# A graph-attention block on one core: the loads of the edge slots written out, with four table entries per register read

## The reference, cut to what matters

```
# N = 1250 nodes, D = 768, 4 heads of C = 192, 3 layers; 41250 edges (src, dst), sorted by dst
loops = arange(N); src, dst = edges plus loops
x1 = relu(x @ W_ah + b_ah)
for each of 3 layers:                                   # gat_conv
    h    = (x1 @ W).reshape(N, 4, 192)
    as_n = (h * a_src).sum(-1);  ad_n = (h * a_dst).sum(-1)
    e    = leaky_relu(as_n[src] + ad_n[dst], 0.2)
    p    = exp(e - segment_max(e, dst)[dst])
    out  = segment_sum(p / segment_sum(p, dst)[dst] * h[src], dst) + b     # then relu
y = relu(concat(3 layers) @ W_out + b_out)
return layernorm(x + y)
```

## Time and profile before

| | |
|---|---|
| median of 3 runs | 987.62 us (987.02 to 990.31) |
| profiled execution, its own time | 989.36 us |
| its span, first to last instruction | 987.1 us |
| mean granted TensorE clock | 0.993 of full speed |
| PE busy | 946.7 us (96% of the span) |
| DVE busy | 742.9 us (75%) |
| ACT busy | 367.7 us (37%) |
| POOL busy | 52.3 us (5%) |

### The profile page before, as it was taken

How to read it: one execution, slowest core, us unless ns; L and a number is a source line. 1 busy time by engine, 2 the same in 40 slices (tenths; PEclk the granted TensorE clock), 3 DMA queues, 4 the chain that set the end, 5 groups by cost and what they waited for, 6 DMA issues and landing times. The chain is left out here.

```text
span 987.1 us, 15188 instructions
## 1 busy us (share of the span) xinstructions
PE 946.7 (96%) x5662; PEld 874.0 (89%) x5662; DVE 742.9 (75%) x1076; ACT 367.7 (37%) x534; POOL 52.3 (5%) x107
## 2 busy tenths in 40 slices
PE   6778899999999999999999999999999999999997
PEld 2556654999999999999999999999999869999996
DVE  6768898699999759997997998988878273234223
ACT  1444532221222234555555465465465461001000
POOL 3333000000000000001001000000010000000000
PEclk9998999999999999999999999999999999999999
DMA  5233272255344381316218136138632173323201
GB/s 167 38 85 87 66 253 77 91 163 157 102 155 136 108 240 54 87 45 130 91 39 166 55 87 121 52 90 262 215 91 66 52 191 112 122 79 109 79 32 31
DMA packets 56347, 108.14 MB, mean 110 GB/s; under 512 B 12669, under 2 KB 39902, under 8 KB 55143
## 3 DMA queue, kind: packets, MB, share of 16 engines
q1 hardware_dynamic: 37460, 66.17, 22.1%
q0 software_dynamic: 5744, 18.82, 8.7%
q10 hardware_dynamic: 13090, 22.44, 7.3%
HBM read 80.34 MB, written 27.08 MB: 109 GB/s over the span
## 5 line engine op out<-in xcount | busy, mean ns | idle before, releaser
L1308 PE MATMUL ps<-R_W 125*125 125x193 f32 x2400 | 397.8, 327 | 5.1 <-ACT R_XIN L720 3.9
L1308 PEld LDWEIGHTS ps<-R_W 125*125 125x125 f32 x2400 | 391.2, 188 | 8.7 <-ACT R_XIN L720 7.6
L705 ACT ACTIVATE R_W<-R_EXP,s 125x1250 f32<-125x1250 f32 x120 | 161.5, 1347 | 161.9 <-PE ps L1308 93.8
L995 DVE SCALAR_TENSOR_TENSOR R_W<-R_W,R_CNT 125x1250 f32<-125x1250 f32 x120 | 174.6, 1455 | 4.3 <-DVE R_EXP L984 2.3
L954 DVE CUSTOM_DVE_ANT_0 R_ROWS<-R_MASK,R_ROWS 125x1250 bf16<-125x1250 bf16 x100 | 138.5, 1456 | 3.2 <-ACTq L658 3.2
L1225 PE MATMUL ps<-Wl_hi,x_hi 128*125 128x384 f32 x360 | 122.1, 339 | 0.0
L1225 PE MATMUL ps<-Wl_hi,x_lo 128*125 128x384 f32 x360 | 121.6, 338 | 0.0
L1225 PE MATMUL ps<-Wl_lo,x_hi 128*125 128x384 f32 x360 | 121.5, 338 | 0.0
L1367 PE MATMUL ps<-Wo_hi,xs_hi 128*125 128x384 f32 (+2 forms) x324 | 109.5, 338 | 0.3 <-PE ps L1357 0.3
L1367 PE MATMUL ps<-Wo_lo,xs_hi 128*125 128x384 f32 (+2 forms) x324 | 109.5, 338 | 0.0
L1367 PE MATMUL ps<-Wo_hi,xs_lo 128*125 128x384 f32 (+2 forms) x324 | 109.2, 337 | 0.0
(11 more groups left out here) (149 smaller groups left out, 898.3 us busy)
## 6 DMA issues: line engine op xcount, KB each, us to landing
xs_dram<-R_XIN POOLq DMA_DIRECT2D x18, 625.0 KB, 10.5
h_dram<-R_HOUT ACTq DMA_DIRECT2D x30, 336.0 KB
R_W<-h_dram SPq DMA_DIRECT2D x12, 840.0 KB
R_ROWS<-as_dram SPq DMA_DIRECT2D x12, 625.0 KB, 4.5
R_EXP<-u_dram SPq DMA_DIRECT2D x6, 1250.0 KB, 6.5
R_X<-u_dram SPq DMA_DIRECT2D x6, 1250.0 KB, 5.7
R_ROWS<-in_W_all SPq DMA_DIRECT2D x18, 384.0 KB, 3.6
Wo_sb<-in_W_out POOLq DMA_DIRECT2D x1, 6912.0 KB, 27.3
```

Of the source, the lines that this page charges most:

```text
L705: nc.scalar.activation(prob[r % PSLOTS], expo[:, r % XSLOTS], ACT.Exp, bias=s02[:, r % NT, ds(2 * p + r // NT, 1)]).then_inc(S["exp_done"], 1)
L995: nc.vector.scalar_tensor_tensor(out=prob[r % PSLOTS], in0=prob[r % PSLOTS], scalar=HUGE, in1=cntT[:, r % NT, 0:N], op0=ALU.min, op1=ALU.m ...
L1308: ins = mm(ps[0:PT, o:o + HW], prob[r % PSLOTS][:, t * PT:(t + 1) * PT], hB[:, q, j], start=(j == 0 and t % 2 == 0), stop=(j == NT - 1), s ...
```

## The change

`load_slot` and its loops are replaced by `load_slots`, which is written out: for each four windows one instruction reads four entries of `table` into four registers, without a check of their values, and then four DMAs follow; no queue loop is left. A batch is now a triple (first, mid, last): SP loads the windows up to mid, POOL the rest. There are seven batches, of 4, 8, 12, 16, 20, 24 and 21 windows, of which SP loads 4, 4, 8, 8, 12, 16 and 12 (64 in all, 52 before) and POOL 0, 4, 4, 8, 8, 8 and 9 (41, before 53). POOL's loads now stand ahead of its 20 `iota`. There are three one-hot buffers instead of two; they fill the space that was kept free at the start of R_EXP and a little more, and `stage_more` moves to R_ROWS.

```diff
-BATCHES = [(0, 4), (4, 8), (8, 16), (16, 28), (28, 40), (40, 54), (54, 70), (70, 88), (88, NW)]
-ONES = 2
+BATCHES = [(0, 4, 4), (4, 8, 12), (12, 20, 24), (24, 32, 40), (40, 52, 60), (60, 76, 84), (84, 96, NW)]
+ONES = 3
...
-        o = KT * HALF
...
-        stage_more, o = view(R_EXP, o, PT, (NT, PT), f16)
...
+        stage_more, _ = view(R_ROWS, o, PT, (NT, PT), f16)
...
-        def load_slot(eng, w, signal):
-
-            start = eng.value_load(table[0:1, ds(w, 1)], min_val=0, max_val=EDGES)
-            eng.dma_start(e8[:, ds(w, 1)].rearrange("p o i s -> p (o i s)"),
-                          edges[ds(start, SLOT)].rearrange("(p i) s -> p (i s)", i=CPW)).then_inc(signal, 16)
+        def load_slots(eng, kind, w0, w1, signal):
+
+            for a in range(w0, w1, 4):
+                z = min(a + 4, w1)
+                _, places = nc.values_load_multi_w_load_instructions(
+                    table[0:1, a:z], engines=[kind], min_val=0, max_val=EDGES,
+                    skip_runtime_bounds_check_because="...")
+                for w, place in zip(range(a, z), places):
+                    eng.dma_start(e8[:, w:w + 1].rearrange("p o i s -> p (o i s)"),
+                                  edges[ds(place, SLOT)].rearrange("(p i) s -> p (i s)", i=CPW)).then_inc(signal, 16)
...
-            for i, (w0, w1) in enumerate(BATCHES):
-                with sp.Fori(w0, (w0 + w1) // 2) as w:
-                    load_slot(sp, w, win_in[i])
+            for i, (w0, mid, w1) in enumerate(BATCHES):
+                load_slots(sp, mybir.EngineType.SP, w0, mid, win_in[i])
...
+            pool.wait_ge(S["table_sb"], 1)
+            for i, (w0, mid, w1) in enumerate(BATCHES):
+                load_slots(pool, mybir.EngineType.Pool, mid, w1, win_in_pool[i])
...
...
-                dve.wait_ge(win_in[i], 16 * ((w0 + w1) // 2 - w0))
-                dve.wait_ge(win_in_pool[i], 16 * (w1 - (w0 + w1) // 2))
+                dve.wait_ge(win_in[i], 16 * (mid - w0))
+                if mid < w1:
+                    dve.wait_ge(win_in_pool[i], 16 * (w1 - mid))
```

More of the change, by code:

```diff
@@ L37 @@
 BLOCKS = CPW // EPR * 2
-BATCHES = [(0, 4), (4, 8), (8, 16), (16, 28), (28, 40), (40, 54), (54, 70), (70, 88), (88, NW)]
-WIDEST = max(z - a for a, z in BATCHES)
-ONES = 2
+BATCHES = [(0, 4, 4), (4, 8, 12), (12, 20, 24), (24, 32, 40), (40, 52, 60), (60, 76, 84), (84, 96, NW)]
+WIDEST = max(z - a for a, m, z in BATCHES)
+ONES = 3
 RING = 250
@@ L334, in acc_cols @@
             return ps[0:PT, o:o + MC]
-        def load_slot(eng, w, signal):
-            start = eng.value_load(table[0:1, ds(w, 1)], min_val=0, max_val=EDGES)
-            eng.dma_start(e8[:, ds(w, 1)].rearrange("p o i s -> p (o i s)"),
-                          edges[ds(start, SLOT)].rearrange("(p i) s -> p (i s)", i=CPW)).then_inc(signal, 16)
+        def load_slots(eng, kind, w0, w1, signal):
[3 more added lines that the diff above has]
+                    table[0:1, a:z], engines=[kind], min_val=0, max_val=EDGES,
+                    skip_runtime_bounds_check_because="the table holds EDGES less GE times a count of groups, 0 to EDGES / GE")
+                for w, place in zip(range(a, z), places):
+                    eng.dma_start(e8[:, w:w + 1].rearrange("p o i s -> p (o i s)"),
+                                  edges[ds(place, SLOT)].rearrange("(p i) s -> p (i s)", i=CPW)).then_inc(signal, 16)
         @block.sync
@@ L523, in _ @@
             ins.then_inc(S["consts_made"], 1)
[L525 to L528, removed]
             pool.wait_ge(S["h_ps"], NT * (PARTS - 1))
```

## The result

The changed kernel takes 964.45 us (median; 963.98 to 965.66), the kernel before 987.63 in the same comparison (987.02 to 990.31): a ratio of 0.9762, with a 95% interval of 0.9742 to 0.9782, so 23.2 us less. The forecast was 965.5.

A forecast was written before the change was run, and what follows sets the result against it. PE was taken to bound all from the scores on, slot-load loops the stage before. Gains of 16.2 (waits), 5.6 (clock) and 1.3 (idle) make 23.1, less 1.0: 987.6 - 22.1 = 965.5 us; range 963 to 968.5, 8 in 10 962.8 to 972.

The forecast's parts named there:

- The bound: From the scores' start at 154.63 us PE bounds everything, busy 818.6 of 832.5 us; the gain is that start's move.
- The cadence: Slot loads in the counting stage: written out, SP issues one per 0.67 us instead of 1.51, POOL 0.85 instead of 1.53.
- The bound from static DMAs, 0.44: Lower limit for SP's time per slot load, 0.44 us, from three static DMAs in a row in 1.31.
- Rival A: Slot loads: SP's cadence is 0.9 to 1.25 us; at 1.0 gain 16, 971 us; at 1.25 gain 2, 985; chance 0.11.
- The rule on register loads: Table reads for slot loads: some 200 ns per register even in bulk, 0.15 more per slot, cadence an estimated 0.82 us.
- PE's need: Counting stage with slots always there: PE needs 71.5 us of the present 93.34, without 16.2 of waits and 5.6 half-clock excess.
- The third buffer: One-hot buffers at changes of batch: a third covers small PE waits, in all 0 to 3 us, counted inside the 71.5.
- Two batches fewer: Counting stage: saves DVE 2.1 us, which PE's work hides, so worth nothing by itself.
- After the units: Between last unit and scores: PE arrives at 131.5, last by 0.9 after DVE's 130.6; scores' start gains 23.1 us.
- Rival C: Behind the faster stage, x's second part is late and PE's clock falls: 3 to 6 of 22 us lost, 970; chance 0.07.
- Rival B: Slot loads: SP stays at 1.51 us a slot with 64 slots, last one-hot 12.4 us slower, 1000 us; chance 0.04.
- Rival D: Slot loads: landings, not issues, were late, so the change does nothing, 987 us; chance 0.02.

The follow-up runs named there:

- the version with moved instructions: The changed kernel with four of DVE's five small integer instructions after batch 0 moved to after batch 3: 964.49 us, run again 964.96 us.
- the kernel with the checked loads: The changed kernel with the loop's body written out, per slot one entry read with its bounds check, then the DMA: 977.86 us, ratio 0.9891.

## Why the prediction was right

- **The bound.** The step that put the whole gain at the start of the scores held: 832.47 us behind it before, 832.44 after.
- **The cadence.** Taken 0.67 on SP, measured 0.64, and 0.67 on POOL, where 0.85 was taken. The bound from static DMAs, 0.44, and the price of one shared read were the right rows. Rival A, 0.9 or more, is ruled out by it.
- **The rule on register loads** did not apply. The trace has 0.302 us for four entries against 0.268 for one, 0.03 for three registers more. By the figure of the Trainium skill ("Runtime: NRT & Kernel Launch", Instruction fetch mechanics) they would cost an estimated 0.6; that page speaks of registers loaded from HBM, and `table` lies on the chip, which the prediction passed over.
- **PE's need.** Predicted 71.5 plus 1.0 of small waits, measured 71.42 with 1.5 of waits in it. Two parts were off and met: PE's busy time fell by 7.2 us (77.14 to 69.90), where the three half-clock stretches account for 5.6. The other 1.6 goes with the waits: in stages without a half-clock stretch PE's busy time is 69.71 with one wait, 69.90 with two, 70.38 with three, 71.31 with nine and 72.04 with eleven, so each wait lengthens it by some 0.2 us on top of its own idle time.
- **The third buffer.** This is the term that was mis-sized: I held it at 0 to 3 us, because I set DVE's 2.4 to 2.7 us against two whole units. It is worth some 6 us (0.9833 to 0.9762 or 0.9769, 0.985 to 0.9792). When DVE has filled its second buffer, PE has been at work on the first for as long as that took. An estimate from the prediction's own numbers: 2 x 1.36 - 1.1 = 1.6 us are left with two buffers and 3.0 with three, against 2.4 to 2.7; units without an x1 step leave less. The sum was not hurt, since the third buffer was in it; the expectation for the writing out alone was, by 4 us.
- **Two batches fewer** were put at nothing. With three buffers they are worth about 2 us; 1.2 of it is seen in the stage (71.33 against 70.14), the rest was not separated.
- **After the units.** PE was to be last at the scores by 0.9, with no idle time. DVE was last, and PE idled 0.49: PE's x1 steps ended at 129.5 and not at 131.5, since the units had ended at 93.4, and DVE's products at 129.8, with a wait of 1.1 us for weights in them. x1's second part was not late, and no wait of PE for it shows. Rival C did not happen.
- **Rival B** was right as a mechanism: with the loop's cadence the new split is 13.0 us slower (1000.8), where 12.4 and 1000 were worked out.
- **Rival D** was right for one wait, the longest, and the sentence "by their loops and not by their bytes" is wrong there. DVE's 4.81 us before 74.25 ended with SP's slot of 67.8:

```profile
L339 SPq DMA_DIRECT2D R_EXP<-in_edges x1: 345/345/345, 67.8 to 67.8; - x1
DMA to landing us min/median/max: 6.5/6.5/6.5
```

ACT had issued x's second part at 67.11. With 1.9 us the slot would have landed at 69.7, and DVE was free at 69.44: some 4.6 of the 12.8 us were the landing's. In the changed kernel SP has issued all its slots by 55.0 and ACT issues this load at 56.36, so the faster cadence also took the slots out of its way. No run moves that load alone with the loops kept, so what that would give is open.
- **Luck.** The forecast did not have PE's start at 21.98 (23.86 before), but little of it reaches the end. With the new batches, three buffers and the new cadence the last unit ended at 93.4 and 93.8 for starts at 21.98 and 21.99, and at 93.8 to 94.2 for starts from 23.80 to 24.10; in the kernel before it ended at 117.2 and 115.3 for starts at 23.86 and 23.99, set by the slots. The 24.7 us between the first two profiles are instead large because the profile before was of an execution 1.7 us above the median. In the timed runs the gain was 23.2 against 22.1. The stage's 71.4 us against 71.5 plus 1.0 is luck in part: 69.9 of work, 1.6 under the forecast, and 1.5 of waits, half a microsecond over it.

## What to carry to other kernels

Before a queue's DMAs are blamed for their bytes, divide the time of a run of issues by its count and compare that with the DMA instruction's own row: here 1.51 against 0.35 us said that the loop around it was the cost. Then work out for each batch by when its data is wanted, and from that the cadence that suffices. Look at the landings too: a small load that goes out just behind a large one can take three times as long (6.4 and 6.5 us here against 1.9), and no cadence shows that. A second edit such as a buffer may be worth nothing before the first and a quarter of the gain after it. Size buffers by what is left in them at the moment the producer turns to other work, and by the consumer's short stretches, and not by their number times its mean.

## What was not expected of the hardware

- PE's ten x1 steps between the edge table and unit 0 (20 matmul records) took 8.65, 9.82, 9.95, 10.02, 10.35, 11.33 or 11.40 us in the profiles, and half clock accounts for the difference. Where they took 10.35 the granted clock is 0.5 for a stretch that begins at 13.6 to 14.2 and ends at 17.0 to 17.6; 3.4 us at half clock cost the 1.7. Where they took 9.82 to 10.02, or 11.33 and 11.40, the views print 1.00, but matmuls and weight loads take up to twice as long (0.34 us for a weight load, 0.19 later) until 16.1 or until 19.2 to 19.4. The traces of those profiles hold no clock record before 16.6 to 17.0 and before 19.5 to 19.8, and the views print 1.00 where there is no record; where the steps took 8.65 the records begin at 11.2 to 11.6. Taking half clock up to the first record gives 1.2 us for the 9.82 (14.20 to 16.59, 1.17 measured) and 2.7 for the 11.33 (14.05 to 19.49, 2.68 measured). So a PEclk of 1.00 ahead of the first record says nothing, and the durations decide. What makes the full clock come sooner or later stays open: PE's order up to there is the same in all of these kernels, yet both of the changed kernel's profiles had 8.65 and both of the version with moved instructions 10.35; the kernel before had 9.82 and 10.35.
- The clock need not fall at the end of the wait that goes before. In the kernel with the checked loads it fell to half at 36.9, as a wait of 3.69 us ended, and the four matmuls behind it took 0.63 us. Behind the wait of 3.43 us that ended at 77.14 the four matmuls took 0.42 at full clock, and the clock fell at 77.9. Before the change it fell at 74.6, inside PE's longest wait.
- Reading four table entries into registers took 0.302 us, one 0.268.
